# An attention and mixture-of-experts layer on one core: the products of zeros that TensorE issues at the ends of the first three query blocks are left out, those at the end of the fourth stay

## The reference

```
x = x + layernorm(attention(layernorm(x)))
x = x + layernorm(moe(layernorm(x)))
```

```
scores = einsum('bhqd,bhkd->bhqk', qs, ks_) * scale     # 192 wide: 128 + 64 rotated
attn = softmax(where(causal, scores, min))
out = einsum('bhqk,bhkd->bhqd', attn, v)  ->  (S, 16 * 128) @ wo
```

## Time and profile before

| | |
|---|---|
| time, median of 3 executions | 1321.38 us |
| lowest and highest of the 3 | 1318.53, 1322.85 us |
| the profiled execution: time, span | 1322.26 us, 1320.5 us |
| TensorE busy in the span | 1170.6 us, 89% |
| VectorE, ScalarE, GpSimd busy | 833.7, 799.0, 735.4 us |
| mean granted clock of TensorE | 0.968 |

### The profile page before, as it was taken

The page is one execution under the profiler, slowest core; times in us unless marked ns, Lnnn a source line. Parts: engine busy times, 40 slices in busy tenths (PEclk is TensorE's granted clock), DMA queues, the critical chain, the costliest instruction groups (busy, mean ns, idle before and its releaser), DMA issues. The chain is left out here.

```text
span 1320.5 us, 19781 instructions
## 1 busy us (share of the span) xinstructions
PE 1170.6 (89%) x6552; PEld 539.8 (41%) x6563; DVE 833.7 (63%) x2104; ACT 799.0 (61%) x1237; POOL 735.4 (56%) x444
## 2 busy tenths in 40 slices
PE   3997999999998999999999899999999999778820
PEld 2633455444443533333333523333333335467610
DVE  6556787666668766665657775667656715745546
ACT  3634662766664566766765467777777783356632
POOL 0045540564654167666776068887778893425545
PEclk9989999999999999999999999999999999989965
DMA  9135300110111010000011001000000000466844
GB/s 280 36 88 132 85 1 1 52 30 17 25 41 33 8 44 21 9 17 17 17 32 40 10 3 57 25 24 6 20 24 25 13 12 17 74 127 207 190 131 135
DMA packets 63031, 70.25 MB, mean 53 GB/s; under 512 B 10080, under 2 KB 52448, under 8 KB 62816
## 3 DMA queue, kind: packets, MB, share of 16 engines
q1 hardware_dynamic: 56656, 56.26, 15.9%
q0 software_dynamic: 4864, 10.51, 3.5%
q10 hardware_dynamic: 1424, 2.38, 0.7%
HBM read 37.51 MB, written 14.83 MB: 40 GB/s over the span
## 5 line engine op out<-in xcount | busy, mean ns | idle before, releaser
L567 POOL TENSOR_TENSOR D<-D,B 128x1024 f32<-128x1024 f32 (+3 forms) x256 | 513.6, 2006 | 136.7 <-ACT B L759 119.2
L759 ACT ACTIVATE B<-ps 128x1024 f32<-128x1024 f32 (+1 forms) x320 | 286.1, 894 | 216.5 <-PE ps L1699 146.3
L1124 DVE TENSOR_REDUCE mxp<-ps 128x1 f32<-128x512 f32 x384 | 263.6, 690 | 192.6 <-PE ps L1673 190.9
L1720 PE MATMUL ps<-B,kv 128*64 128x512 f32 (+3 forms) x1280 | 304.0, 555 | 2.7 <-ACT C L646 2.4
L646 ACT ACTIVATE ps<-D 128x1024 f32<-128x1024 f32 (+3 forms) x327 | 288.3, 883 | 24.1 <-DVE D L1142 14.5
L1699 PE MATMUL ps<-A,KTh 128*128 128x512 f16 (+3 forms) x768 | 209.6, 355 | 2.7 <-ACT ps L646 2.7
L560 POOL TENSOR_TENSOR D<-B 128x1024 f32<-128x1024 f32 (+1 forms) x32 | 71.0, 2219 | 224.3 <-ACT B L759 224.3
L1126 DVE CUSTOM_DVE_ANT_0 ps<-ps,c 128x128 f32<-128x128 f32 (+3 forms) x256 | 127.0, 497 | 60.6 <-PE ps L1673 56.3
L1673 PE MATMUL ps<-KTh,A 128*128 128x512 f16 (+3 forms) x384 | 136.2, 358 | 8.2 <-DVE mxp L1124 7.0
L1699 PE MATMUL ps<-A,KTl 128*128 128x512 f16 (+3 forms) x384 | 136.0, 354 | 0.0
L1699 PEld LDWEIGHTS ps<-A,KTh 128*128 128x128 f16 x768 | 66.1, 98 | 101.5 <-issue 51.8
(11 more groups left out here) (273 smaller groups left out, 1792.3 us busy)
## 6 DMA issues: line engine op xcount, KB each, us to landing
results<-B SPq DMA_DIRECT2D x64, 128.0 KB
xnTl<-in_L_ffn_experts_gate_up SPq DMA_DIRECT2D x16, 256.0 KB, 2.7
A<-in_L_attn_wq SPq DMA_DIRECT2D x4, 768.0 KB, 21.4
B<-in_L_attn_x SPq DMA_DIRECT2D x5, 512.0 KB, 5.7
D<-in_L_attn_wo SPq DMA_DIRECT2D x2, 1024.0 KB, 21.4
A<-C SPq DMA_DIRECT2D x16, 128.0 KB, 2.3
A<-C SPq DMA_DIRECT2D x32, 64.0 KB, 2.0
A<-stg SPq DMA_DIRECT2D x16, 128.0 KB, 2.3
```

The costliest lines, as they stand in the source:

```text
L567: nc.gpsimd.tensor_tensor(acc[:, :, c0:], acc[:, :, c0:], Pr[:, kt % P_RING, :, c0:], ALU.add).then_inc(sum_done, 1)
L759: nc.scalar.activation(Pr[:, kt % P_RING, :, c0:], ps[:, 2 * (kt % ST_RING):2 * (kt % ST_RING) + 2, c0:], ACT.Exp, scale=SM_SCALE).then_in ...
L1124: V.tensor_reduce(most, rough, AX.X, ALU.max).then_inc(mx_free, 1)
L1720: ins = T.matmul(ps[LORA * s:LORA * (s + 1), BK_O, c0:], kv[:, kt, 0:LORA], Pr[:, kt % P_RING, s, c0:], start=(kt == 0), stop=(kt == KT - 1))
```

## The change

`stay_busy` is not called any more at the ends of blocks 0, 1 and 2. At the end of block 3 it is called with the same numbers, 16, 10 and 3, and the four calls behind that block are as they were. Waits, semaphores and the other engines' programs are the same. 3 x 18 = 54 products and their weight loads go.

```diff
                 if qc < NC - 1:
                     prime(0)
-                stay_busy(5 if qc < NC - 1 else 16)
+                if qc == NC - 1:
+                    stay_busy(16)
                 pe.wait_ge(l_done, CR_L + (qc + 1) * NP)
...
                 pe.wait_ge(o_free, CR_O + (qc + 1) * NP)
 
-                stay_busy(10)
+                if qc == NC - 1:
+                    stay_busy(10)
                 pe.wait_ge(terms_ready, qc + 1)
...
                 ins.then_inc(turned_ready, 1)
-                stay_busy(3)
+                if qc == NC - 1:
+                    stay_busy(3)
                 pe.wait_ge(inv_ready, qc + 1)
```

## The result

The changed kernel takes 1340.42 us (median of 4 runs, 1339.8 to 1343.5) where the kernel before, beside it, takes 1319.95 us (4 runs, 1317.94 to 1322.85). The ratio is 1.0148, 95% interval 1.0122 to 1.0174: slower by 1.5%, 20 us, where I had forecast 2 us and no measurable change.

A forecast was written before the change was run, and what follows sets the result against it. TensorE, busy for 89% of the span, was taken to bound the kernel. Three ends at 0.8 us less 0.4 us given back made +2.0 us on 1321.38, so 1323.4 us, with a range of 1320.0 to 1327.1.

The forecast's parts named there:

- the 0.43 us: End of block 2: the first five zeros delay the denominators' weight load by this much; removal gives 0.4 us back, once.
- the 205.2 to 207.9: End of block 0: earliest and latest moment at which TensorE's clock would fall, counted from the starts of two waits.
- It is low for 3.4 us: Block ends: length of the half-clock stretch after the clock falls, taken from low stretches elsewhere in the trace.
- 0.8 us for an end: Ends of blocks 0 to 2: cost of the lost clock, the middle of an early fall (0.4) and a late one (1.2).
- The price of a turn: Loop of spreads and first output products: a turn takes 1.63 us at half clock instead of 0.96.
- the number of turns: Loop, late fall: 2.4 us at half clock hold 1.47 turns and not 2.5, so 1.0 us is lost.
- the bound of 1.7 us for an end: Block ends: most that one low stretch can cost, half of 3.4 us, if all of it were products in line.
- The clock stays up: Rival at the block ends: pauses too short to lose the clock, 1321.0 us; 0.14, including a fall at only one end.
- the pause rule of the Trainium skill: TensorE loses its clock only above a stated pause length; the longest pause left stays below it, so nothing would be lost.
- The low clock costs twice as much: Rival at the loop of spreads and first output products: an end costs 1.7 us, sum +4.7, 1326.1 us; chance 0.20.
- the 6.6 us at 0.50: Trace from 68.0 to 74.6 us: TensorE, just back at work, kept at half clock for longer than 3.4 us.
- The other low stretches move: Rival at 102, 757 and 771 us: low stretches shift, each worth up to 1.7 us; over 4 us faster, chance 0.04.

The follow-up runs named there:

- the run without the third three zeros: Kernel before, leaving out only the three zeros ahead of the first spread at the ends of blocks 0 to 2: 1337.66 us, ratio 1.0147.
- the one without the ten: Kernel before, leaving out only the ten zeros ahead of the turn of the terms at the ends of blocks 0 to 2: 1340.83 us, ratio 1.0160.

## Why the prediction was wrong

**Right.** The removal itself: the pauses are 1.06, 2.31 and 0.68 us (1.1, 2.2, 0.7 forecast), and the real products start where they did behind their inputs. At block 2 the reduction now ends at 740.96 + 1.23 = 742.19 and the denominators load at 742.24: the 0.43 us came back. The clock falls at all three ends, at 207.4 in the first, within the 205.2 to 207.9 that I gave. The lateness goes through the pairs in full (282.75 us of them before and after). The sign was forecast, and for the right reason.

**The step that failed** is "It is low for 3.4 us". The three low stretches that I had read all stood in dense products of 128 rows, and behind each, at 105.5, 760.9 and 774.6, the clock was back at 1.00. I carried their length over to a place with other work behind it. At the ends stand spreads of 48 rows and output products with gaps between them, and 13.6 to 20.4 us passed at 0.50. The term "0.8 us for an end" is 6.6 us measured (19.7 / 3). At each end six turns of the loop take 0.75 us more each, 4.5 us in all. The rest, 0.8, 3.1 and 2.3 us, is in what stands around them, at the last two ends most of it in the output products behind the loop. The price of a turn was nearly right (1.63 forecast, 1.71 measured), and the number of turns, 1.47, was not. With it fell the bound of 1.7 us for an end, which took one low stretch of 3.4 us for granted.

**The rivals.** "The clock stays up" is refuted, and with it the pause rule of the Trainium skill (TensorE: Matmul & The Clock Gate, "Why this matters for your kernels") as a safe bound: the longest pause here was 2.31 us, and in the run without the third three zeros the only empty place of the three was 0.68 us long. The prediction counted one place where the trace did not agree with that rule, the wait of 2.02 us; those of 2.75 and 2.82 us are short of its length too, and the clock was low behind them as well. "The low clock costs twice as much" named the right place, the loop, and the right doubt, the 6.6 us at 0.50. I gave it 0.20, priced only the 1.7 us, and argued against more with the sentence that a second low stretch needs TensorE to be idle in the first. That is wrong: TensorE was busy for 13.24 of 13.60 us of the stretch at the first end. "The other low stretches move" happened, but all that lies outside the ends differs by 1.1 us together.

**A sign that I passed over.** 68.0 to 74.6 is 6.6 us at 0.50 with 5.31 us busy. It said that a TensorE busy for most of the time may stay low for more than 3.4 us. I named it in a rival and gave it no price.

## What to carry to other kernels

Idle products that keep TensorE's clock are priced by what stands behind them: if that is dense work of all rows, a lost clock costs a few products (3.4 us at half clock, in the rows before); if it is small work with gaps, the clock stays low until denser work comes, here at some 6 us an end ((1337.66 - 1319.56) / 3) for a pause that shows as 0.7. Read the granted clock of the stretch behind a wait, not the busy row, and fill with products that use all 128 rows. Where the real products use fewer rows, padding them with rows of zeros can help to keep the clock, at no column more; here it took the place of the third three, and it did not bring a lost clock back.

## What the runs showed of the hardware that was not expected

TensorE's clock fell behind 7.13 us of busy records in 7.70 when the fillers used 48 rows, and did not with fillers of 128 rows and 64 columns. Half the columns changed nothing that could be measured (1321.9 us against 1322.18), 48 rows lost most of what the zeros gave (1336.99 and 1336.22 us, where the changed kernel takes 1340.42). All fillers were products of zeros; whether others would do better was not tried.

The clock also fell in a part that no edit touched, and not in every execution. In the profiled run with zeros of 128 rows and 64 columns the preparation of weights was at half clock, in that of the kernel before it was not. Busy by stretch, of that run and then of the kernel before:

```profile
42.80:59.90 17.10, 17.10 (x60) 11.05 (x60) 7.73 (x15) 5.12 (x15) 0.00 (x0) 0.50 0.10 32
```

```profile
42.80:59.90 17.10, 17.10 (x103) 11.15 (x102) 10.75 (x21) 10.21 (x30) 0.00 (x0) 1.00 0.10 32
```

60 records against 103 in the same 17.1 us, with TensorE "busy" in all of it. The end of block 0 then begins at 209.15 instead of 202.54 us. Of the 15 profiled executions one more had this, the one without the ten. Such falls may be a part of why the runs of the kernel before lie up to 12.2 us apart in one comparison (1316.86 to 1329.03 us); that was not followed up.
